# Second attention: score matmuls of 64 rows in two row groups, exponentials of two heads in one instruction, one ring of three banks for everything else

## The chip, the cores and the metric

The kernel runs on one core of a Trainium2 chip. The metric is the device time of one execution, in microseconds (us). A measurement of this kernel can tell a difference of some 0.3% from none.

## The reference

Input x has 4 batches of 1024 tokens with 128 features, all in float32. Four blocks follow one another, each added to x after a layer norm of x: a first attention with relative positions (8 heads), a feed-forward with a choice of two of eight experts, the second attention, and the same feed-forward again. The change is in the second attention. It has 16 query heads of 8 features and one key and one value head that all of them share:

```python
q = x @ Wq + bq
k = x @ Wk + bk
v = x @ Wv + bv
q = q.reshape(b, t, NUM_HEADS, HEAD_DIM)
scores = jnp.einsum('bthd,bsd->bhts', q, k) / jnp.sqrt(jnp.float32(HEAD_DIM))
mask = jnp.tril(jnp.ones((t, t), dtype=scores.dtype))
scores = scores * mask - 10000000000.0 * (1.0 - mask)
probs = jax.nn.softmax(scores, axis=-1)
out = jnp.einsum('bhts,bsd->bthd', probs, v)
out = out.reshape(b, t, NUM_HEADS * HEAD_DIM)
return out @ Wo + bo
```

## The kernel before, in words

**Layout.** The kernel is one program with five engine streams: SyncE (`sync`, line 343), GpSimd called POOL (445), TensorE (491), ScalarE (794) and VectorE (968). Each stream walks through the same lists of work units, `plan_a` for the first attention, `plan_f(0)`, `plan_b` for the second attention, `plan_f(1)`. A unit is a tuple such as `("b_s", b, g, ch, J, q)`. Engines meet through semaphores that count up. PSUM, TensorE's output memory, has eight banks of 512 float32 columns; `bank_free` holds for each bank the semaphore value that says that its reader is done.

**How a head fits the array.** Each number of queries and keys is split into a high part in float32r and a low rest, so that products of float32r matmuls come out in float32 accuracy. A head takes 32 of 128 partitions: 8 rows each for the products high times high, low times high and high times low, and two rows for the row maximum that is taken off. A group g has four heads q = 0 to 3 on partitions 32q to 32q+31. There are 4 batches b with 4 groups g, 16 head groups in all. The query tile `Q` holds all four heads of a group. The key tile `K` has four copies for each batch, one for each q, in which only the 32 partitions of q are filled and all others are zero (line 462 zeroes the tile once, lines 932 to 942 fill the blocks on ScalarE). So a matmul over all 128 rows gives the scores of head q alone.

**The units of a head group.** `b_in` (692) projects 512 tokens by three matmuls into bank 7, for g = 0 to 3 the queries, for g = 4 the keys. ScalarE takes the bank out twice, as `y` with bias and scale and as `yh` in float32r (lines 927 and 931); VectorE makes the mix of high and low parts in `b_in2` (1303 to 1317). `b_keys` copies the key blocks. `b_vals` (704) makes the values. `b_max` (712) makes scores for 128 queries of head q against up to 512 keys, into one of banks 0, 1, 2 in turn; VectorE reduces each to a row maximum (1328 to 1343), with a custom instruction that adds the causal mask where the tile has the diagonal, with a plain reduction elsewhere. There are 48 a group. `b_shift` and `b_shift2` (1344 to 1364) put the negated maxima into the spare rows of `Q` through PE transposes in bank 7. `b_s` (735) makes the scores the other way round, 128 keys (J) against up to 512 queries (half ch), into one of banks 3, 4, 5 in turn; ScalarE takes the exponential into `P`, a ring of `NP` = 7 tiles (943 to 952); POOL zeroes the upper triangle of the 128 diagonal columns where J is in the half (479 to 487). There are 48 of these a group too, four for each of twelve (ch, J), and eight of the twelve have a diagonal. `b_pv` (747) multiplies the four heads' `P` with the values in four matmuls of 128 rows and 32 columns, which write the four partition quadrants of bank 6. Columns of ones beside the eight of the values give the sum of the exponentials in the same matmul. `b_norm` copies the sums out on ScalarE, `b_norm2` (764, 1365) transposes them in bank 7 and VectorE divides. After the fourth group `b_out` and `b_out2` apply the output projection, also in bank 7. Layer norm pieces (`ln_turn`) and gate logits (`gt_logits`) of the next feed-forward run inside the stage, in bank 7.

**The order.** `plan_b` (165 to 234) writes the order by hand. `finish(n)` is the main list of head group n: three scores, then the value product of the key tile before, then the fourth score. `prepare(n+1)` is the side list: projections and maxima of the next group. The first `AHEAD` = 15 maxima of the group after that are kept to cover `b_shift` and `b_shift2` in `chain`. A loop (226 to 232) puts side units between main units so that both lists end together, by prices that stand in `cost` and `price`, one side unit at a time:

```python
            while i >= 4 and side and spent * total < goal * done:
                h = side.pop(0)
                out.append(h)
                spent += cost(h)
```

`first(b)` is the projection of the keys and of group 0 of batch b, spread into the side list of the last group of the batch before. For b = 0 it runs alone at the start of the stage, and then all maxima of group 0.

## Time and profile before

| what | value |
|---|---|
| median of 3 runs | 2920.83 us (2916.55 to 2924.42) |
| profiled execution, its own time | 2921.59 us |
| its span, first to last instruction | 2919.9 us |
| granted TensorE clock, mean | 0.952 of full speed |
| busy TensorE / VectorE / ScalarE / POOL | 2631.4 / 2041.6 / 1656.7 / 355.0 us |
| exponentials of the second attention (L952) | 768, 327.7 us |
| maximum matmuls (L721), score matmuls (L741) | 768 and 768 |

How to read it. Busy time of an engine is the union of its instructions' records. TensorE's matmuls overlap in the records, so that a busy TensorE is not an array at its peak: how far apart two matmuls start says what one costs. Times on the timeline count from the first instruction of the span. PE is TensorE's matmul, PEld its weight load, DVE is VectorE, ACT is ScalarE. L741 is line 741 of the kernel. A tile `ps` is PSUM, `r_K`, `r_Q`, `r_P`, `r_mx` are the tiles of the text above.

### The profile page before, as it was taken

How to read it: one execution, taken by the hardware profiler on the slowest of the kernel's cores; microseconds unless marked ns; L12 is line 12 of the kernel's file. 1: busy time of each engine (PE TensorE's matmuls, PEld its weight loads, DVE VectorE, ACT ScalarE, POOL GpSimd, SP SyncE). 2: the span in 40 equal slices, each digit the busy share in tenths (PEclk: the TensorE clock that was granted, in tenths of full speed). 3: DMA queues.
4: the chain of work that ended last, by engine and by line, in shares of the span. 5: the costliest groups of instructions: out<-in, count | busy, mean ns of one | idle time of the engine just before them, and what ended most of it. 6: DMA issues, size and time to landing. Idle time of an engine off the chain costs nothing.

```text
span 2919.9 us, 45160 instructions
## 1 busy us (share of the span) xinstructions
PE 2631.4 (90%) x14496; PEld 2047.8 (70%) x14496; DVE 2041.6 (70%) x5231; ACT 1656.7 (57%) x3430; POOL 355.0 (12%) x782
## 2 busy tenths in 40 slices
PE   2899999999999999999997079988998989998998
PEld 1688788888888888888886067765555555554777
DVE  3576776767767677677664078869777776773887
ACT  2566666666666666666664044544666656565454
POOL 0000000000000000000000123321221221222344
PEclk9999999999999999999999589978999999999999
DMA  2655556566655566556663100000000000000000
GB/s 84 206 203 205 183 200 209 200 214 207 211 205 201 205 214 214 205 195 205 214 208 110 51 6 1 1 1 1 1 1 1 1 1 1 1 1 1 9 8 15
DMA packets 98467, 321.63 MB, mean 110 GB/s; under 512 B 11556, under 2 KB 25508, under 8 KB 98020
## 3 DMA queue, kind: packets, MB, share of 16 engines
q1 hardware_dynamic: 98234, 318.74, 31.9%
q8 instruction: 119, 1.95, 0.3%
q14 instruction: 114, 0.93, 0.1%
HBM read 158.53 MB, written 157.29 MB: 108 GB/s over the span
## 4 chain that ended last, share of the span: by engine, by line
PE 77%; DVE 11%; ACT 5%; SPq 3%; issue 3%; DMA 1%; POOL 0%; DVEq 0%; ACTq 0%; POOLq 0%
PE ps L238 7%; PE ps L240 7%; PE ps L239 7%; PE ps L608 7%; PE ps L583 5%; PE ps L582 5%; PE ps L721 4%; PE ps L759 4%; PE ps L621 4%; PE ps L623 4%; PE ps L622 4%; PE ps L653 4%; PE ps L741 4%; PE ps L654 4%; PE ps L655 4%
## 5 line engine op out<-in xcount | busy, mean ns | idle before, releaser
L874 ACT ACTIVATE a_Ph<-ps 128x512 fp32r<-128x512 f32 x512 | 305.9, 597 | 474.5 <-PE ps L608 474.4
L1177 DVE CUSTOM_DVE_ANT_0 a_sp<-ps,a_sp 128x1024 f32<-128x1024 f32 x256 | 313.3, 1224 | 184.8 <-PE ps L240 178.9
L952 ACT ACTIVATE r_P<-ps 128x512 f32<-128x512 f32 (+3 forms) x768 | 327.7, 491 | 187.5 <-PE ps L741 183.2
L1183 DVE TENSOR_TENSOR a_Pl<-ps,a_Ph 128x512 fp32r<-128x512 f32 x512 | 349.3, 682 | 10.1 <-ACT a_Ph L874 9.8
L582 PE MATMUL ps<-a_fa,a_ua 128*128 128x384 f32 (+2 forms) x960 | 327.2, 353 | 5.0 <-DMA a_ub<-a_ua 2.6
L903 ACT ACTIVATE r_y<-ps 128x256 f32<-128x256 f32 x512 | 194.4, 385 | 220.9 <-PE ps L655 215.0
L867 ACT ACTIVATE a_sp<-a_sp,a_nm 128x1024 f32<-128x1024 f32 x256 | 295.0, 1152 | 29.4 <-DVE a_nm L1177 29.3
L608 PE MATMUL ps<-ident,a_sp 128*128 128x128 f32 x2048 | 309.0, 273 | 0.0
L653 PE MATMUL ps<-r_Wh,p_xh 128*128 128x512 f32 x512 | 223.0, 436 | 92.1 <-DVE r_Wl L1212 44.6
L721 PE MATMUL ps<-r_K,r_Q 128*128 128x512 f32 (+3 forms) x768 | 281.9, 402 | 18.0 <-DVE r_mx L1339 12.6
L608 PEld LDWEIGHTS ps<-ident,a_sp 128*128 128x128 f32 x2048 | 250.7, 141 | 61.6 <-issue 0.4
L583 PE MATMUL ps<-a_fb,a_ub 86*128 86x384 f32 (+2 forms) x960 | 290.9, 318 | 0.0
L1339 DVE CUSTOM_DVE_ANT_0 ps<-ps,maskq 128x256 f32<-128x256 f32 (+3 forms) x512 | 244.8, 506 | 54.2 <-PE ps L721 53.3
L741 PE MATMUL ps<-r_Q,r_K 128*128 128x512 f32 (+3 forms) x768 | 253.0, 374 | 30.2 <-ACT r_P L952 28.4
L859 ACT ACTIVATE a_rt<-ps 128x384 f32<-128x384 f32 x512 | 251.2, 491 | 10.5 <-PE ps L583 9.6
L721 PEld LDWEIGHTS ps<-r_K,r_Q 128*128 128x128 f32 x768 | 144.8, 198 | 157.9 <-DVE r_mx L1339 80.9
L473 POOL TENSOR_TENSOR r_acc<-r_acc,r_yk 128x256 f32<-128x256 f32 x256 | 189.4, 740 | 333.7 <-DVE r_yk L1244 322.8
L621 PE MATMUL ps<-a_Ph,a_nath 128*128 128x512 f32 x512 | 214.0, 418 | 15.9 <-DVE a_Pl L1183 15.9
L485 POOL TENSOR_SCALAR_AFFINE_SELECT r_P<-r_P 128x128 f32<-128x128 f32 x512 | 152.2, 307 | 556.3 <-ACT r_P L952 547.7
L1343 DVE TENSOR_REDUCE r_mx<-ps 128x1 f32<-128x512 f32 x256 | 176.2, 688 | 50.6 <-PE ps L721 49.3
L654 PE MATMUL ps<-r_Wl,p_xh 128*128 128x512 f32 x512 | 209.9, 410 | 0.0
L655 PE MATMUL ps<-r_Wh,p_xl 128*128 128x512 f32 x512 | 209.5, 409 | 0.0
(203 smaller groups left out, 5631.0 us busy)
## 6 DMA issues: line engine op xcount, KB each, us to landing
scr<-a_rt SPq DMA_DIRECT2D x256, 576.0 KB, 3.1
a_sp<-scr SPq DMA_DIRECT2D x256, 512.0 KB, 4.4
a_wc<-wsp SPq DMA_DIRECT2D x24, 512.0 KB, 5.5
wsp<-a_wc SPq DMA_DIRECT2D x8, 512.0 KB, 4.6
a_ub<-a_ua SPq DMA_DIRECT2D x64, 44.0 KB
x<-in_q SPq DMA_DIRECT2D x4, 512.0 KB, 15.9
wst<-in_w1t SPq DMA_DIRECT2D x8, 256.0 KB
out<-x SPq DMA_DIRECT2D x4, 512.0 KB, 3.2
```

The costliest lines, as they stand in the source:

```text
L582: e.matmul(out, self.ua[:, s, side, qs], self.fa[:, base + a:base + z], start=True, stop=False)
L583: i = e.matmul(out, self.ub[:, s, side, qs], self.fb[:, base + a:base + z], start=False, stop=True)
L608: i = e.transpose(ps[:, 4 + j % 2, 128 * k:128 * k + 128], self.sp[:, (4 * qd + k) % NSP, 128 * j:128 * j + 128], ident[:, :])
L621: e.matmul(OB, self.nath[:, s, j, :], self.Ph[:, slot, :], start=j == 0, stop=False)
L653: e.matmul(hb, self.xh[:, cs], self.Wh[:, k, :], start=True, stop=False)
L654: e.matmul(hb, self.xh[:, cs], self.Wl[:, k, :], start=False, stop=False)
L655: e.matmul(hb, self.xl[:, cs], self.Wh[:, k, :], start=False, stop=True).then_inc(S["f_mm"], 1)
L721: e.matmul(ps[:, bank, 0:w], self.Q[:, b % 2, g, 128 * I:128 * I + 128], self.K[:, b % 2, q, 512 * part:512 * part + w], start=True, stop= ...
L741: e.matmul(ps[:, bank, off:512], self.K[:, b % 2, q, 128 * J:128 * J + 128], self.Q[:, b % 2, g, 512 * ch + off:512 * ch + 512], start=Tru ...
L952: e.activation(self.P[:, pt, off:512], ps[:, bank, off:512], ACT.Exp).then_inc(S["b_exp"], 1)
L1177: e.tensor_tensor_reduce(out=w, in0=ps[:, 2:4, :].rearrange("p a n -> p (a n)"), in1=w, scale=-1.0, scalar=3e38, op0=ALU.add, op1=ALU.min, ...
L1183: e.tensor_tensor(self.Pl[:, n % 3, :], ps[:, 4 + n % 2, :], self.Ph[:, n % 3, :].bitcast(F32), ALU.subtract).then_inc(S["p_lo"], 1)
```

## The change

The kernel after differs in the second attention and in what prepares it:

1. **Keys.** `K` has `KV` = 2 copies for each batch instead of 4. Copy v holds the keys in the 32-partition blocks q with q % 2 = v, and zeros in the others. VectorE writes the mixed keys into a new tile `Kf`, and POOL makes both copies by a multiplication with a mask column (`lowmask`), two instructions of 512 columns for each half of a batch. The zeroing of `K` and ScalarE's `b_keys` go.
2. **Matmuls.** A maximum or score matmul of head q contracts 64 rows: partitions 0 to 63 for q = 0, 1, and 64 to 127 for q = 2, 3. The maxima go in the order q = 0, 2, 1, 3, so that neighbours are in different row groups. The width and the number of matmuls stay.
3. **Scores in pairs.** A unit `b_s` has two heads, pr and pr + 2, in banks 2 and 3 (pr = 0) or 4 and 5 (pr = 1). One ACTIVATE takes the exponential of both banks, `P` has 4 slots of two tiles, and POOL masks both tiles in one instruction. The order in `finish` is pair, pair, value product of the key tile before.
4. **Ring.** `b_max`, `b_in`, `b_vals`, `b_shift2`, `b_norm2`, `b_out` and `b_out2` take banks 0, 1, 7 in turn, in the order of the plan. `ln_turn` and `gt_logits` stay in bank 7. A `b_in2` is put off until its bank or its result is wanted. The side list gives two maxima at a time.
5. **Projection.** ScalarE reads the bank once, and multiplies by a mask column with a bias that has been multiplied beforehand, so that `yh` has the high part only in the rows that need it. VectorE takes it from the bank itself. The scale 1/sqrt(8) is applied to the weights once, in `b_prepare`.

```diff
-NP = 7
+NP = 4
+KV = 2
...
-        m = [("b_max", b, g, I, q, part) for I in range(7, -1, -1) for q in range(4) for part in range(1 + I // 4)]
-        q = [(u, b, g + 1, half) for u in ("b_in", "b_in2") for half in range(2)] if g < 3 else first(b + 1) if b + 1 < B else []
+        m = [("b_max", b, g, I, q, part) for I in range(7, -1, -1) for part in range(1 + I // 4) for q in (0, 2, 1, 3)]
+        q = [("b_in", b, g + 1, half) for half in range(2)] if g < 3 else first(b + 1) if b + 1 < B else []
...
-                r += [("b_s", b, g, ch, J, q) for q in range(3)] + prev + [("b_s", b, g, ch, J, 3)]
+                r += [("b_s", b, g, ch, J, 0), ("b_s", b, g, ch, J, 1)] + prev
...
-            while i >= 4 and side and spent * total < goal * done:
-                h = side.pop(0)
-                out.append(h)
-                spent += cost(h)
+            while i >= 2 and side and spent * total < goal * done:
+                for h in side[:2] if [v[0] for v in side[:2]] == ["b_max"] * 2 else side[:1]:
+                    out.append(side.pop(0))
+                    spent += cost(h)
...
+    ring, at, held, done = (0, 1, 7), 0, {}, []
+    for u in out:
+        shares = u[0] in ("b_in", "b_vals", "b_max", "b_shift2", "b_norm2", "b_out", "b_out2")
+        bank = ring[at % 3] if shares else 7 if u[0] in ("ln_turn", "gt_logits") else None
+        while bank in held or held and u[0] == "b_max" and [v for v in held.values() if v[2] in (u[2], 4)]:
+            done.append(held.pop(next(iter(held))))
+        done.append(u + (bank,) if shares else u)
+        at += shares
+        if u[0] == "b_in":
+            held[bank] = ("b_in2",) + u[1:] + (bank,)
...
+                        for v in range(KV):
+                            e.tensor_scalar(self.K[:, b % 2, v, os], self.Kf[:, half, :].bitcast(F32),
+                                            self.lowmask[:, 2 + v:3 + v], None, ALU.mult).then_inc(S["b_keys"], 1)
...
-                        e.affine_select(out=self.P[:, pt, off:off + 128], in_=self.P[:, pt, off:off + 128],
-                                        compare_op=ALU.is_ge, fill=0.0, pattern=[[1, 128]], channel_multiplier=-1,
+                        e.affine_select(out=self.P[:, slot, :, off:off + 128], in_=self.P[:, slot, :, off:off + 128],
+                                        compare_op=ALU.is_ge, fill=0.0, pattern=[[0, 2], [1, 128]], channel_multiplier=-1,
...
-                e.matmul(ps[:, bank, 0:w], self.Q[:, b % 2, g, 128 * I:128 * I + 128],
-                         self.K[:, b % 2, q, 512 * part:512 * part + w], start=True, stop=True).then_inc(S["b_mmm"], 1)
+                rows = slice(32 * (q - q % KV), 32 * (q - q % KV + KV))
+                e.matmul(ps[:, bank, 0:w], self.Q[rows, b % 2, g, 128 * I:128 * I + 128],
+                         self.K[rows, b % 2, q % KV, 512 * part:512 * part + w], start=True, stop=True).then_inc(S["b_mmm"], 1)
...
+                for k in range(2):
+                    bank, q = 2 + 2 * pr + k, pr + 2 * k
+                    rows = slice(32 * (q - q % KV), 32 * (q - q % KV + KV))
+                    e.wait_ge(*free[bank])
+                    i = e.matmul(ps[:, bank, off:512], self.K[rows, b % 2, q % KV, 128 * J:128 * J + 128],
+                                 self.Q[rows, b % 2, g, 512 * ch + off:512 * ch + 512], start=True, stop=True)
+                    free[bank] = S["b_exp"], nst
+                i.then_inc(S["b_smm"], 1)
...
-                e.activation(self.P[:, pt, off:512], ps[:, bank, off:512], ACT.Exp).then_inc(S["b_exp"], 1)
+                e.activation(self.P[:, slot, :, off:512], ps[:, bank:bank + 2, off:512], ACT.Exp).then_inc(S["b_exp"], 1)
...
-                e.activation(self.y[:, k, :], ps[:, 7, :], ACT.Identity, bias=self.bq[:, g:g + 1],
-                             scale=DB ** -0.5 if g < 4 else 1.0).then_inc(S["b_y"], 1)
...
-                e.activation(self.yh[:, k, :], self.y[:, k, :], ACT.Copy).then_inc(S["b_yh"], 1)
+                e.activation(self.yh[:, k, :], ps[:, bank, :], ACT.Identity, bias=self.bl[:, g:g + 1],
+                             scale=self.lowmask[:, m:m + 1]).then_inc(S["b_yh"], 1)
...
-                e.scalar_tensor_tensor(dst, self.yh[:, k, :].bitcast(F32), self.lowmask[:, m:m + 1], self.y[:, k, :],
-                                       ALU.mult, ALU.add).then_inc(S["b_y2"], 1)
+                e.scalar_tensor_tensor(dst, ps[:, bank, :], self.bq[:, g:g + 1], self.yh[:, k, :].bitcast(F32),
+                                       ALU.add, ALU.subtract).then_inc(S["b_y2"], 1)
```

## Rows read from the trace of the kernel before

**Rows 1.** Timeline of the head: start us, length us, engine, line, tiles

```profile
1949.90 0.73 PE L238 MATMUL ps<-p_xh,r_wh 128*128 128x512 f32 x1
...
1966.17 4.29 PE L721 MATMUL ps<-r_K,r_Q 128*128 128x512 f32 x7
```

**Rows 2.** Windows view: engines' busy us (instructions), clock, DMA share, GB/s, by stretch

```profile
core 0: us, PE busy (x) PEld busy (x) DVE busy (x) ACT busy (x) POOL busy (x), PEclk, DMA share, GB/s
1949.00:1966.00 17.00, 12.38 (x42) 9.14 (x41) 3.30 (x5) 10.06 (x16) 0.00 (x0) 0.50 0.00 0
1970.00:2006.00 36.00, 33.18 (x97) 19.32 (x96) 34.22 (x108) 7.61 (x14) 1.31 (x5) 0.71 0.00 1
2006.00:2636.00 630.00, 575.06 (x3445) 336.02 (x3443) 476.56 (x1617) 394.88 (x865) 141.76 (x475) 0.97 0.00 1
2636.00:2670.00 34.00, 27.07 (x166) 11.35 (x166) 2.26 (x8) 22.62 (x53) 9.09 (x32) 1.00 0.00 1
```

**Rows 3.** Timeline of the tail, one key tile of full width

```profile
2657.62 1.06 PE L759 MATMUL ps<-r_P,r_V 128*32 128x512 f32 x8
...
2658.62 0.97 PE L741 MATMUL ps<-r_Q,r_K 128*128 128x512 f32 x3
2659.16 2.07 ACT L952 ACTIVATE r_P<-ps 128x512 f32<-128x512 f32 x4 [0.55 <-PE ps L741]
...
2659.81 0.50 PE L741 MATMUL ps<-r_Q,r_K 128*128 128x512 f32 x1 [0.22 <-ACT r_P L952]
...
2660.24 1.06 PE L759 MATMUL ps<-r_P,r_V 128*32 128x512 f32 x8
```

**Rows 4.** Waits view, 2006 to 2636 us: total us, times, longest us

```profile
ACT r_P L952 <- PE ps L741: 175.8, 154, 4.2
...
DVE ps L1339 <- PE ps L721: 53.3, 70, 3.2
...
DVE r_mx L1343 <- PE ps L721: 47.6, 53, 3.2
```

**Rows 5.** Timeline around a value product with maxima beside it

```profile
2627.19 0.28 PE L721 MATMUL ps<-r_K,r_Q 128*128 128x256 f32 x1
...
2627.40 1.06 PE L759 MATMUL ps<-r_P,r_V 128*32 128x512 f32 x8
2627.51 0.43 DVE L1339 CUSTOM_DVE_ANT_0 ps<-ps,maskq 128x256 f32<-128x256 f32 x1
...
2628.40 0.50 PE L721 MATMUL ps<-r_K,r_Q 128*128 128x256 f32 x2
...
2628.82 0.43 DVE L1339 CUSTOM_DVE_ANT_0 ps<-ps,maskq 128x256 f32<-128x256 f32 x1 [0.82 <-PE ps L721]
```

**Rows 6.** TensorE groups by form, 2006 to 2670: busy us, mean ns, idle before

```profile
L759 PE MATMUL ps<-r_P,r_V 128*32 128x512 f32 x768 | 104.0, 613 | 2.0 <-ACT r_P L952 0.7
```

**Rows 7.** Groups of ScalarE by form, 2006 to 2670 us

```profile
L952 ACT ACTIVATE r_P<-ps 128x512 f32<-128x512 f32 x384 | 206.3, 599 | 129.2 <-PE ps L741 128.5
...
L952 ACT ACTIVATE r_P<-ps 128x128 f32<-128x128 f32 x124 | 30.6, 276 | 7.0 <-PE ps L741 4.9
...
L931 ACT ACTIVATE r_yh<-r_y 128x512 fp32r<-128x512 f32 x33 | 20.8, 631 | 1.1
...
L941 ACT ACTIVATE r_K<-r_yk 32x512 fp32r<-32x512 f32 x24 | 15.0, 624 | 0.4
```

**Rows 8.** Costliest groups of the page: an exponential of 1024 columns

```profile
L867 ACT ACTIVATE a_sp<-a_sp,a_nm 128x1024 f32<-128x1024 f32 x256 | 295.0, 1152 | 29.4 <-DVE a_nm L1177 29.3
```

**Rows 9.** Groups of VectorE, 2006 to 2636 us

```profile
L1339 DVE CUSTOM_DVE_ANT_0 ps<-ps,maskq 128x256 f32<-128x256 f32 (+1 forms) x472 | 224.6, 504 | 54.2 <-PE ps L721 53.3
L1343 DVE TENSOR_REDUCE r_mx<-ps 128x1 f32<-128x512 f32 x231 | 159.0, 688 | 48.8 <-PE ps L721 47.6
```

**Rows 10.** Groups of POOL, 1949 to 2670 us

```profile
L485 POOL TENSOR_SCALAR_AFFINE_SELECT r_P<-r_P 128x128 f32<-128x128 f32 x512 | 152.2, 307 | 556.3 <-ACT r_P L952 547.7
```

**Rows 11.** Timeline of POOL before the first feed-forward

```profile
1607.04 1.26 POOL L461 TENSOR_TENSOR wst<-wst,wr 128x512 f32<-128x512 f32 x1 [1604.70 <-DMA wr<-in_w1r]
```

224 lines of the change are left out of this document (109 added, 115 removed).

## The prediction, as it was made before the kernel ran

> **What bounds the kernel now.** I read the page first, for where the second attention lies, then the windows view of its stretches, the waits in the long one, the groups of VectorE, and the timeline of two spots. The stage runs from the first query and key projection at 1949.9 us [rows 1] to about 2670 us, 720 of 2919.9 us; nothing else of the program is changed by more than a microsecond or two. It has four stretches [rows 2]. A head of projections (1949 to 1966). A filling phase (1970 to 2006), in which TensorE has only row-maximum matmuls to do and VectorE reduces them: it is busy 34.22 of 36 us. The long stretch, 630 us, in which 15 of the 16 head groups get scores, exponentials and value products while the next group's maxima are made. And a tail of 34 us with the last group's scores and hardly any VectorE work.
>
> In the long stretch VectorE is busy 476.56 us, ScalarE 394.88, and TensorE 575.06; but TensorE's records overlap, so its 91% is not array time. The array's demand comes from start to start: a group of three score matmuls of 512 columns takes 0.97 us where one takes 0.50, so (0.97 - 0.50)/2 = 0.235 us each [rows 3]. One value product (four heads, eight records) keeps the array 1.0 us, from 2657.62 to 2658.62. Per head group the maxima and the scores each have 36 full widths of 512 columns (4608 columns for each of four heads), so 72 x 0.235 = 16.9 us; value products have 9 full widths, 9.0 us; the projections (7.5 matmuls, 1.8 us), four sets of four transposes (each at most as long as a value product, so up to 4) and small ones give some 6. That is 32 us of 630/15 = 42.0. VectorE's demand is 476.6/15 = 31.8 us. Neither engine is full: both lose about 10 us a group to each other. The waits view says how: VectorE stood 53.3 + 47.6 us for maximum matmuls, ScalarE 175.8 us for score matmuls [rows 4]. The timeline shows the usual case [rows 5]: a value product starts at 2627.40 and holds TensorE until 2628.40, VectorE finishes the maxima that were ready, and gets the next at 2628.82, after 0.82 us idle. VectorE's whole idle time is 630 - 476.6 = 153.4 us, 10.2 a group, 0.85 for each of its 12 value products. So the stage is bound by an in-order TensorE that alternates between banks freed by two other engines, with TensorE and VectorE nearly level in demand.
>
> **The change, part by part.**
>
> **Matmuls of 64 rows.** The 1536 maximum and score matmuls stay as many and as wide, but neighbours use rows 0-63 and 64-127 and different banks. If such a pair runs at once, the 16.9 us fall to 8.5 at best. No row of this trace has two row groups. The nearest is the value product, whose four heads use four column groups: 613 ns a record and eight records in 1.06 us [rows 3, 6], so they do run at once. Bounds: 8.5 us off a group, or nothing, or less than nothing by switches; I take 8.5 for the scores' half and for the maxima count it as hidden, since a pair there starts together only where both banks are free. The Trainium skill, page TensorE: Matmul & The Clock Gate, section on packing small matmuls, has row groups start about 4 ns apart; by it the full 8.5 us would go, which is the same sum, and no row here shows it.
>
> **Mode switches.** In the rows a value product's 1.0 us is all that can hold a switch in and out, and there are still 12 a group. New are switches between 64-row matmuls and full ones: about 8 other units a group. I price two switches at 0.1 us each, 1.6 us a group, from a full-width score before a value product (2659.81 to 2660.24, 0.43 us) [rows 3]: over its 0.235 that is 0.2, part of it a wait; zero is the other end. It lies on TensorE, which then has 32 - 8.5 + 1.6 = 25 us of demand and room for it. The Trainium skill, page TensorEngine Tiling (Array Packing), section Key Properties, says that changing the tiling mode drains the engine. By it with TensorE still the bound, 15 x 1.6 = 24 us would be given back.
>
> **Exponentials in pairs.** 768 become 384. By length, 599 ns for 512 columns and 276 for 128 [rows 7] give 0.84 ns a column and 0.168 us fixed, so 1.03 us for 1024. Four in a row took 2.07 us, spaced (2.07 - 0.60)/3 = 0.49 [rows 3], so a lower bound is 0.92; the upper is 1.15, the 1024-wide exponential of the first attention [rows 8]. I take 1.03. Also off ScalarE go the second copy of each projection (631 ns x 40) and the 32 copies of keys (624 ns) [rows 7], 45 us in the stage. ScalarE is at 63% in the long stretch, so none of this is on the path by itself.
>
> **Four banks for scores, three for all else.** Scores wait for the exponential of the same pair one key tile earlier. Maxima keep three banks but share them with projections, transposes and outputs (some 10 turns a group), and are issued two at a time. What a projection holds: its bank until ScalarE's pass and VectorE's subtraction; VectorE waits for ScalarE, which may have one 1.03 us exponential ahead of it. Before it was covered by two units between them; now by two bank turns, two maxima of about 0.55 us (224.6 + 159.0 over 703) [rows 9]. I count 0.5 us x 2.5 a group.
>
> **Masks and keys on POOL.** The 512 masks of 307 ns [rows 10] become 256 of twice the elements: between 0.31 and 0.61, I take 0.45. It stands in the way of the eight diagonal value products of a group by 0.15 us at most, beside maxima that TensorE still has. The key copies, 16 on 512 columns, at most the 1.26 us of the two-input subtraction [rows 11]: POOL is 77% idle [rows 2], but masks queue behind them, and a value product behind those: 6 halves x 2.5 = 15 us as the outer bound in the long stretch, 0 the other; I take 3, since the wait of POOL comes with maxima still to do. The memset of the key tile at the first feed-forward's start goes; POOL waits there anyway, so nothing; neither does the scaling of the weights, one VectorE instruction and one ScalarE wait in the first feed-forward, once.
>
> **The steady sum.** What VectorE does per group is unchanged (the projection's subtraction reads a bank in place of a tile). The question is its idle time. From the last pair of maxima before a value product to the next that VectorE gets: 0.235 for a pair of scores, 1.0 for the product, 0.42 from issue to VectorE's start (2628.40 to 2628.82) [rows 5], 1.66 us. The stock at that point is up to three maxima, 3 x 0.55 = 1.6, where now two or fewer were left. So 0.1 to 0.4 idle a product; I take 0.22, 2.6 us a group, and 2.4 for projections, keys and the group's end, where the shift is made of the last maxima. That is 5.0 in place of 10.2: 15 x 5.2 = 78 us less. ScalarE's demand becomes some 22 us a group (12 pairs of full width at 1.03, four each of 384, 256 and 128 columns at 0.81, 0.60 and 0.38, and 3 for projections and sums), TensorE's 25: both stay below the 36.8 that VectorE then needs.
>
> **Tail.** There a key tile of full width takes 2.62 us (2657.62 to 2660.24), of which ScalarE idles 0.55 [rows 3]: a third bank is not enough over a value product. With two pairs the exponentials can follow each other, 2 x 1.03 = 2.06. Six full tiles x 0.56 = 3.4; I take 3.
>
> **Head.** From 1949.90 to the first maximum at 1966.17 [rows 1] are 16.3 us, one projection after the other through one bank. With three banks, four projections of three matmuls and the values can run on, about 12 us: 4 less, from 0 to 6.
>
> Sum: 78 + 3 + 4 = 85 us off the profiled execution's 2921.6; it is 0.8 above the median of 2920.83. Forecast 2836.
>
> **Bounds of the sum.** Best: VectorE idles only as in the filling phase, 1.78 us on 34.22 [rows 2], 25 us in the long stretch, 128 saved there, 10 at the ends: 2783. Worst of this case: it is 80% busy, 596 us, 34 saved and 3 at the ends: 2884.
>
> **Rivals.**
> **VectorE saturated.** The stock of three covers the product nearly always: 2783 to 2800. For it: the filling phase. Against: the products are 1.0 us and the widths of 128 reduce in a third of the time of a full one.
> **Row groups one after the other, or switches that eat the gain.** TensorE keeps 32 us plus up to 1.6 of demand, level with VectorE. Only the paired exponentials and fuller stock help; idle falls to 7.5 us a group, 15 x 2.7 = 40 saved, 5 at the ends: 2876. For it: no row shows row groups together. Against: column groups do.
> **Nothing moves.** The shared ring's waits (0.5 us and more at 10 turns) give back what the pairs bring: 2915 to 2925.
> **Slower: TensorE's clock.** A less busy array might be granted 1.2 GHz for long. It was granted 0.97 in the long stretch, 0.71 in the filling phase [rows 2]. At half clock 25 us of demand become about 49, over the 42.0 of now. With a share f of half clock a group takes 36.8 + 12.2 f: it decides from f = 0.43; at 0.6 it is 44.1, 32 us worse in all, less 7 at the ends: 2946. Against: the tail, with scores and products only and gaps between them, ran at 1.00.
>
> **How the numbers follow.** The forecast 0.60, VectorE saturated 0.12, row groups in series 0.16, nothing moves 0.04, clock 0.08. The first three are faster, 0.88. The range goes from the best bound to a little over the third case, 2782 to 2888, and leaves out the clock and the no-change case. 0.3% (9 us) is about what a measurement of this kernel can tell from no change.
>
> **What would show it.** Right: pairs of score matmuls that start within tens of ns; VectorE at 83 to 90% of the long stretch, which is about 550 us; 384 exponentials, about 1.03 us at full width; full tiles of the tail at about 2.1 us; a granted clock as before. Wrong: a pair spaced 0.235 us, VectorE's waits for maximum matmuls above 80 us still, long waits of VectorE for the projection's ScalarE pass, or a clock under 0.8.

## The result, and the profile after

The change makes the kernel **slower**: 3016.49 us (median of 4 runs, 3014.02 to 3023.82) against 2918.69 for the kernel before beside it, ratio 1.034 with an interval of 1.031 to 1.036. Forecast was 2836 us, faster by 2.9%. The profiled execution took 3014.02 us, its span is 3011.6 us, and the mean granted TensorE clock fell from 0.952 to 0.897. The clock has two levels here, 1.2 and 2.4 GHz, so that a mean of 0.75 is half of the time at the lower one; that share is called the half-clock share below.

The clock by slices of the page, kernel after. The second attention lies in the 26th to the 37th of the 40 slices:

```profile
PEclk9999999999999999999995799956976778768999
```

The windows view of the kernel after answers to [rows 2]: filling phase, long stretch, tail, then one head group, and the same units of the next batch:

```profile
core 0: us, PE busy (x) PEld busy (x) DVE busy (x) ACT busy (x) POOL busy (x), PEclk, DMA share, GB/s
1970.00:2006.00 36.00, 29.66 (x67) 15.93 (x68) 29.70 (x95) 2.84 (x3) 0.00 (x0) 0.50 0.00 0
2006.00:2730.00 724.00, 636.31 (x3447) 311.74 (x3447) 483.37 (x1617) 336.13 (x453) 114.62 (x252) 0.75 0.00 1
2730.00:2756.00 26.00, 23.36 (x170) 8.88 (x172) 3.03 (x8) 20.03 (x27) 6.41 (x16) 0.93 0.00 1
2151.60:2188.40 36.80, 31.54 (x216) 14.83 (x214) 29.09 (x92) 20.62 (x28) 6.40 (x16) 1.00 0.00 1
...
2352.40:2398.40 46.00, 42.35 (x215) 19.59 (x214) 29.52 (x92) 20.82 (x28) 6.45 (x16) 0.67 0.00 1
```

And the windows view of the kernel before, of the group with the same units as the last two:

```profile
2128.90:2166.30 37.40, 35.14 (x218) 20.31 (x216) 29.23 (x92) 23.52 (x53) 9.64 (x32) 1.00 0.00 1
```

Three things are in these lines. The long stretch is 724 us where 630 were before and 550 forecast, at a clock of 0.75 where it was 0.97: half of it at 1.2 GHz. The same head group takes 36.80 us at full clock and 46.00 us at 0.67, while what VectorE, ScalarE and POOL have to do in it is the same (29.09 and 29.52 us, 20.62 and 20.82, 6.40 and 6.45); only TensorE's records grow. And at full clock this group takes 36.80 us against 37.40 before: the change gains 0.6 us there, not 5.2.

One group doesn't stand for all. Timed in both traces from the first exponential of a group to the first of the next, with the half-clock share in brackets:

| head groups, in order | before, us | after, us |
|---|---|---|
| 3 and 11 | 46.4 (0.15), 47.0 (0.15) | 42.8 (0.16), 44.2 (0.15) |
| 4, 8 and 12 | 37.7, 37.8, 37.7 (0 each) | 36.8 (0), 46.0 (0.67), 37.6 (0.09) |
| 6, 10 and 14 | 46.4, 45.9, 48.0 (0.07, 0.07, 0.14) | 63.2, 63.6, 63.7 (0.76, 0.70, 0.86) |
| 15 | 31.3 (0) | 26.3 (0) |

Where the clock is the same, the change gains between 0.9 and 5.0 us a group. Groups 6, 10 and 14 lose 16 to 18 us each, with the highest half-clock shares. In the order of the plan they are the groups among whose units stand the layer norm pieces and gate logits of the next feed-forward, which keep to bank 7, now one of the ring's three. With 128-row matmuls and nearly the full clock (the first experiment below) they still take 53.5, 56.3 and 51.5 us, so a part of their loss is not the clock.

The groups by form, kernel after, from 1950 to 2760, answer to [rows 6, 7, 9, 10, 11]:

```profile
L964 ACT ACTIVATE r_P<-ps 128x1024 f32<-128x1024 f32 x192 | 191.4, 1023 | 186.5 <-PE ps L767 185.3
L744 PE MATMUL ps<-r_K,r_Q 64*128 64x512 f32 x384 | 161.3, 592 | 52.9 <-DVE r_Q L1329 34.9 <-DVE r_mx L1352 5.7 <-DVE p_xl L1039 3.2
L786 PE MATMUL ps<-r_P,r_V 128*32 128x512 f32 x768 | 121.3, 709 | 0.7 <-ACT r_P L964 0.6
L509 POOL TENSOR_SCALAR_AFFINE_SELECT r_P<-r_P 128x256 f32<-128x256 f32 x256 | 102.6, 407 | 611.2 <-ACT r_P L964 609.1
L501 POOL TENSOR_SCALAR r_K<-r_Kf,lowmask 128x512 fp32r<-128x512 f32 x16 | 24.8, 1564 | 62.1 <-DVE r_Kf L1329 62.1
```

The single prices were right where a row had been near: 1023 ns for two heads' exponentials (1.03 taken), 407 ns for a double mask (0.45 taken). A value product's record grew from 613 [rows 6] to 709 ns; in the two like groups above it is 605 ns at full clock and 757 at 0.67, so that goes with the clock. The key copies are dearer than their upper bound, 1.56 us for at most 1.26.

The waits from 2006 to 2730, kernel after, answer to [rows 4]:

```profile
ACT r_P L964 <- PE ps L767: 322.6, 197, 19.3
DVE ps L1352 <- PE ps L744: 112.5, 92, 4.4
...
PEld ps L744 <- DVE r_Q L1329: 46.0, 24, 3.3
...
DVE r_mx L1356 <- PE ps L744: 43.3, 57, 1.9
```

VectorE stands 156 us for maximum matmuls where it stood 101, and ScalarE 323 where it stood 176. A new wait is TensorE's for L1329, the projection's step on VectorE, in whose bank the next maximum has to go. The timeline shows it once, at full clock:

```profile
2153.77 0.39 PE L249 MATMUL ps<-p_xl,r_wh 128*128 128x512 f32 x1
2154.33 0.50 PE L744 MATMUL ps<-r_K,r_Q 64*128 64x512 f32 x2
2154.44 0.78 ACT L953 ACTIVATE r_yh<-ps,r_bl,lowmask 128x512 fp32r<-128x512 f32 x1 [1.72 <-PE ps L250]
2156.07 0.74 DVE L1329 SCALAR_TENSOR_TENSOR r_Q<-ps,r_bq,r_yh 128x512 fp32r<-128x512 f32 x1
2156.86 0.51 PE L744 MATMUL ps<-r_K,r_Q 64*128 64x512 f32 x2 [0.59 <-DVE r_Q L1329]
2157.39 1.29 DVE L1356 TENSOR_REDUCE r_mx<-ps 128x1 f32<-128x512 f32 x2 [0.59 <-PE ps L744]
```

TensorE gives two maxima at 2154.33 and the next two only at 2156.86, right after L1329 ends; VectorE then waits 0.59 us for them. The two matmuls of a line start together (x2 in 0.50 us, as long as one), so the row groups do run at once.

The tail came out as predicted, or better. The timeline between two full-width value products in it:

```profile
2748.10 2.98 ACT L964 ACTIVATE r_P<-ps 128x1024 f32<-128x1024 f32 x3
2749.74 1.06 PE L786 MATMUL ps<-r_P,r_V 128*32 128x512 f32 x8
2751.27 2.95 ACT L964 ACTIVATE r_P<-ps 128x1024 f32<-128x1024 f32 x3 [0.19 <-PE ps L767]
2751.66 1.06 PE L786 MATMUL ps<-r_P,r_V 128*32 128x512 f32 x8
```

From one product to the next it is 1.92 us, against 2.62 before [rows 3] and 2.06 forecast.

### The profile page after: what moved, and what is told of

Its sections match the earlier page's. It is cut to its first block, busy times and chain, and to the rows that moved or that the text cites. A ratio compares the mean times of both kernels' runs of the same rounds, so it can differ in the third digit from the quotient of the medians.

```text
span 3011.6 us, 43744 instructions
## 1 busy us (share of the span) xinstructions
PE 2684.2 (89%) x14496; PEld 2015.9 (67%) x14496; DVE 2049.5 (68%) x5234; ACT 1584.7 (53%) x2974; POOL 322.6 (11%) x541
## 3 DMA queue, kind: packets, MB, share of 16 engines
q8 instruction: 117, 1.92, 0.3%
## 4 chain that ended last, share of the span: by engine, by line
PE 77%; DVE 11%; ACT 4%; SPq 3%; issue 3%; DMA 1%; POOL 0%; DVEq 0%; POOLq 0%; ACTq 0%
PE ps L248 7%; PE ps L250 7%; PE ps L249 7%; PE ps L632 7%; PE ps L744 6%; PE ps L786 5%; PE ps L607 4%; PE ps L606 4%; PE ps L645 4%; PE ps L647 4%; PE ps L646 4%; PE ps L677 3%; PE ps L678 3%; PE ps L679 3%; PE ps L767 3%
## 5 line engine op out<-in xcount | busy, mean ns | idle before, releaser
L964 ACT ACTIVATE r_P<-ps 128x1024 f32<-128x1024 f32 (+3 forms) x384 | 298.3, 809 | 329.6 <-PE ps L767 328.0
L744 PE MATMUL ps<-r_K,r_Q 64*128 64x512 f32 (+3 forms) x768 | 287.7, 518 | 79.9 <-DVE r_Q L1329 40.0
L744 PEld LDWEIGHTS ps<-r_K,r_Q 64*128 64x128 f32 x768 | 146.8, 242 | 264.8 <-DVE r_mx L1352 79.8
L786 PE MATMUL ps<-r_P,r_V 128*32 128x512 f32 (+3 forms) x1536 | 208.4, 623 | 5.5 <-ACT r_os L970 4.6
L248 PE MATMUL ps<-p_xh,a_gah 128*128 128x512 f32 x512 | 206.2, 403 | 2.0 <-DVE a_nm L1191 2.0
L1256 DVE SCALAR_TENSOR_TENSOR r_yk<-ps,p_comb,r_y 128x256 f32<-128x256 f32 x384 | 182.9, 480 | 34.0 <-ACT r_y L929 19.7
```

The lines of the kernel that those rows point to most:

```text
L248: e.matmul(out, lh, rh, start=True, stop=False)
L744: e.matmul(ps[:, bank, 0:w], self.Q[rows, b % 2, g, 128 * I:128 * I + 128], self.K[rows, b % 2, q % KV, 512 * part:512 * part + w], start= ...
L786: i = e.matmul(ps[32 * q:32 * q + 32, 6, off:512], self.V[:, b % 2, J, :], self.P[:, (got - 2 + q % 2) % NP, q // 2, off:512], start=J == ...
```

## The experiments: which part costs

Eighteen kernels ran. Ratios are to the kernel before on the same chip, with 95% intervals; the clock is the mean of the one profiled execution, whose time can lie at the edge of the others (for 128 rows it was the fastest of four, 2944.6 us).

| kernel | rows | us | ratio (interval) | clock |
|---|---|---|---|---|
| after | 64 | 3016.5 | 1.034 (1.031 to 1.036) | 0.897 |
| after with 128-row matmuls | 128 | 2952.4 | 1.011 (1.009 to 1.013) | 0.952 |
| after, neighbours in one row group | 64 | 3072.9 | 1.052 (1.050 to 1.055) | 0.883 |
| before with 64-row matmuls alone | 64 | 3022.0 | 1.034 (1.032 to 1.036) | 0.896 |

**128 rows, all else of the change kept.** The key tile has four copies again. For room, `yh` and `Kf` lie over tiles of the feed-forward, with the waits that this needs. POOL makes twice as many key copies, and neighbouring matmuls can't run at once any more.

```diff
-KV = 2
+KV = 4
...
-        self.yh = sb("yh", [128, 2, 512], F32R)
+        self.yh = self.y[:, :, :].bitcast(F32R)
...
-        self.Kf = sb("Kf", [128, 2, 512], F32R)
+        self.Kf = self.yk[:, :, :].bitcast(F32R)
```

> The changed kernel with the score and maximum matmuls back at 128 rows (four zero-padded key copies), everything else of the change kept: pairs of heads per exponential, two maxima at a time, the ring of banks 0, 1, 7. Theory A (score pairs that run at once leave the array idle, and the clock is granted at 1.2 GHz for that): the granted clock of the stage goes back to 0.93 or more, and the time to 2830 to 2900, since a fit of the 15 head groups of the changed kernel against their share of half clock gave 34.8 us at full clock against 39.8 before. Theory C (the shared ring's waits make the loss and the gaps): the clock stays under 0.85 and the time at 2990 to 3050.

Measured: 2952.38 us, 1.0109 (1.0088 to 1.0131). The windows view of its long stretch:

```profile
2008.00:2664.00 656.00, 581.76 (x3474) 347.61 (x3472) 483.88 (x1623) 337.83 (x456) 133.30 (x264) 0.96 0.00 1
```

With 128 rows the clock is back at 0.96, and two thirds of the loss are gone. But 1.1% stays, so the rest of the change costs something as well, and the 2830 to 2900 us that theory A expected did not come. Its ground was a line fitted through the 15 groups, 34.8 us at full clock against 39.8. Such a line mixes groups of different work: it prices the half clock at some 32 us a group, where like groups give 13.9 (worked out below).

**The 64-row matmuls with neighbours in the same row group.** Heads in the order 0, 1, 2, 3, so that neighbours cannot run at once.

```diff
-        m = [("b_max", b, g, I, q, part) for I in range(7, -1, -1) for part in range(1 + I // 4) for q in (0, 2, 1, 3)]
+        m = [("b_max", b, g, I, q, part) for I in range(7, -1, -1) for part in range(1 + I // 4) for q in range(4)]
...
-                    bank, q = 2 + 2 * pr + k, pr + 2 * k
+                    bank, q = 2 + 2 * pr + k, 2 * pr + k
```

> The changed kernel, with the heads ordered 0, 1, 2, 3, so that neighbouring matmuls of 64 rows share a row group and can't run at once. Theory A (idle time of the array): the clock comes back to 0.93 or more and the time is as that of the kernel with 128 rows, within 1%. Theory B (a matmul of 64 rows counts for less, whether or not it overlaps): the clock stays at 0.7 to 0.8 and the time is above the changed kernel's 3016, at 3030 to 3100, since the matmuls now take their full time at the low clock. Theory C: little moves, 3016 to 3050.

Measured: 3072.87 us, 1.0525 (1.0501 to 1.0549), clock 0.883. This is theory B's range. Running two at once is worth 56 us here, a part of which may be the somewhat lower clock. It is not the overlap that lowers the clock: without it, it is lower still.

**The row change alone, on the kernel before.** The lines shown are those of the maxima; the score matmuls are changed in the same way, and the heads go in the order 0, 2, 1, 3.

```diff
-        self.K, self.V = sb("K", [128, 2, 4, L], F32R), sb("V", [128, 2, 8, 32])
+        self.K, self.V = sb("K", [128, 2, 2, L], F32R), sb("V", [128, 2, 8, 32])
...
-                e.matmul(ps[:, bank, 0:w], self.Q[:, b % 2, g, 128 * I:128 * I + 128],
-                         self.K[:, b % 2, q, 512 * part:512 * part + w], start=True, stop=True).then_inc(S["b_mmm"], 1)
+                rows = slice(64 * (q // 2), 64 * (q // 2) + 64)
+                e.matmul(ps[:, bank, 0:w], self.Q[rows, b % 2, g, 128 * I:128 * I + 128],
+                         self.K[rows, b % 2, q % 2, 512 * part:512 * part + w], start=True, stop=True).then_inc(S["b_mmm"], 1)
```

> The kernel before, with the matmuls of 64 rows in two row groups alone (head order 0, 2, 1, 3, two key copies), one exponential a head, the old rings of three banks. Theories A and B: the clock of the stage falls below 0.88 and the time is above before, 2940 to 3020. Theory C (the ring): no ring here, so the time is at or below before's 2919, down to 2870, with the clock above 0.93.

Measured: 3022.01 us, 1.0339 (1.0315 to 1.0363), clock 0.896. The row change alone gives the whole loss; the clock of its long stretch is 0.76. The parts don't add: rows alone 3.4%, the rest alone 1.1%, both together 3.4%. Under the 64-row clock the rest costs nothing more.

## The experiments: the clock

**A filler of 128 rows.** One more matmul of 128 rows and the same width ahead of each maximum matmul, its product overwritten.

```diff
+                e.matmul(ps[:, bank, 0:w], self.Q[:, b % 2, g, 128 * I:128 * I + 128], self.K[:, b % 2, q % KV, 512 * part:512 * part + w],
+                         start=True, stop=True)
                 e.matmul(ps[:, bank, 0:w], self.Q[rows, b % 2, g, 128 * I:128 * I + 128],
```

> The changed kernel with one more matmul of 128 rows and the same width in front of each maximum matmul, into the same bank, overwritten by it: 768 more matmuls, work that nobody needs. It adds 36 x 0.235 = 8.5 us of array time a head group at full clock. Theory A and B: the clock of the stage rises to 0.9 or more and the kernel gets faster than 3016 in spite of more work, 2880 to 2960. Theory C: the clock is not what costs, and the time goes up to 3030 to 3120.

Measured: 3612.46 us, 1.237 (1.234 to 1.239), clock 0.816. Both theories failed. The timeline of TensorE shows what was overlooked, at half clock and at full clock:

```profile
2199.58 0.80 PE L744 MATMUL ps<-r_K,r_Q 128*128 128x512 f32 x1
2200.31 0.79 PE L746 MATMUL ps<-r_K,r_Q 64*128 64x512 f32 x1
2201.03 0.79 PE L744 MATMUL ps<-r_K,r_Q 128*128 128x512 f32 x1
...
2206.97 0.50 PE L746 MATMUL ps<-r_K,r_Q 64*128 64x512 f32 x1
2207.39 0.50 PE L744 MATMUL ps<-r_K,r_Q 128*128 128x512 f32 x1
2207.83 0.50 PE L746 MATMUL ps<-r_K,r_Q 64*128 64x512 f32 x1
```

Neighbours of different tile shape start 0.72 us apart at half clock and 0.43 at full clock, for 512 columns that take 0.235 between equals. The filler had brought far more changes of shape: counted in the traces over the stage, some 1850 against 510 in the kernel after. So it says nothing of the clock by itself. Why its clock was low as well (0.60 from 2052 to 3349) was not found.

**A filler that changes no shape**, and its control on the kernel before: each maximum matmul issued twice, with the same rows and to the same bank.

```diff
+                e.matmul(ps[:, bank, 0:w], self.Q[rows, b % 2, g, 128 * I:128 * I + 128],
+                         self.K[rows, b % 2, q % KV, 512 * part:512 * part + w], start=True, stop=True)
                 e.matmul(ps[:, bank, 0:w], self.Q[rows, b % 2, g, 128 * I:128 * I + 128],
```

> The kernel after the change, with each of the 768 maximum matmuls of 64 rows issued twice in the same row group and to the same bank: twice the array work of the maxima, and no new change of tile shape between neighbours (the filler before it doubled those changes, and cannot speak for the clock alone). If the granted clock follows how much of the time the array works, whatever the rows, it rises above the 0.897 of after, and the time stays at 3016 or falls, as low as 2960. If work in 64 rows is what the clock does not count as full work, the clock stays at 0.88 to 0.90 and the time only gains the added columns, 768 x 0.23 to 0.46 us = 177 to 353 us of array work of which a third to a half shows: 3070 to 3190 us.

> The kernel before, with each maximum matmul of 128 rows issued twice: the control of the 64-row run with doubled maxima, which cost 0.6% over after and brought its clock from 0.897 to 0.915. If there the array's added work was paid for by clock that came back, the same doubling here, where the clock is 0.95 already, has little to win back and costs more: 3 to 6%, 3010 to 3090 us, clock 0.95 or above. If the array's time is simply not what bounds either kernel, it costs about the same 0.6% here: 2930 to 2945.

Measured: on after 3034.05 us, 1.0381 (1.0359 to 1.0403), clock 0.915; on before 2992.02 us, 1.0243 (1.0228 to 1.0258), clock 0.962. The long stretches, in the windows view of the one and of the other kernel:

```profile
2014.00:2765.00 751.00, 674.57 (x4175) 382.41 (x4173) 489.15 (x1622) 340.02 (x455) 115.02 (x252) 0.83 0.00 1
```

```profile
2000.00:2700.00 700.00, 667.71 (x4158) 445.42 (x4155) 495.14 (x1622) 407.17 (x867) 143.44 (x480) 0.99 0.00 1
```

The same number of matmuls more, 768, cost the kernel before 72 us and the kernel after 18 us (in the profiled executions the long stretch grows by 70 and by 27 us). In the second the clock of the stretch rises from 0.75 to 0.83, in the first there was little to win, from 0.97 to 0.99. This is a strong sign that the clock costs the time and doesn't merely go with it. It is not a proof: TensorE of the kernel after also waits more, and may hide more of the added work. The first run fell between its two ranges, the control cost less than the 3 to 6% expected.

**Streams without pauses.** Five streams of 512 columns on TensorE alone, put after the second attention of the kernel before.

```diff
+        for kind, count in ((0, 800), (1, 800), (2, 1600), (0, 400), (3, 600)):
+            for k in range(count):
+                half = 0 if kind == 1 else k % 2
+                rows = slice(0, 128) if kind == 0 or kind == 3 and k % 2 else slice(64 * half, 64 * half + 64)
+                e.matmul(ps[:, 0 if kind == 1 else k % 2, :], self.K[rows, 1, 0, 0:128],
+                         self.Q[rows, 1, 3, 0:512], start=True, stop=True)
```

> The kernel before, with five streams of matmuls of 512 columns put on TensorE alone after the second attention, while the other engines wait: 800 of 128 rows, 800 of 64 rows in one row group, 1600 of 64 rows in alternating row groups, 400 of 128 rows, 600 alternating between 128 and 64 rows. If the clock falls for work in 64 rows as such: 1.00 in the first and fourth stream, 0.5 in the second, and between in the third, where two run at once. If it falls for pauses of the array: 1.00 in the first four and below 1 in the fifth, where each change of shape leaves a gap. A change of shape costs 0.2 us by the filler run: the fifth takes 600 x 0.43 = 258 us at full clock, against 600 x 0.22 = 132 us without it.

Windows view, one line in the middle of each stream: 128 rows; 64 rows in one row group; 64 rows in two; 128 rows; 128 and 64 in turn:

```profile
2700.00:2870.00 170.00, 170.00 (x734) 137.82 (x733) 0.00 (x0) 0.00 (x0) 0.00 (x0) 1.00 0.00 1
2880.00:3055.00 175.00, 175.00 (x755) 139.22 (x754) 0.00 (x0) 0.00 (x0) 0.00 (x0) 1.00 0.00 1
3065.00:3240.00 175.00, 175.00 (x1509) 140.12 (x1508) 0.00 (x0) 0.00 (x0) 0.00 (x0) 1.00 0.00 1
3250.00:3335.00 85.00, 85.00 (x367) 68.91 (x366) 0.00 (x0) 0.00 (x0) 0.00 (x0) 1.00 0.00 1
3345.00:3590.00 245.00, 245.00 (x579) 106.94 (x579) 0.00 (x0) 0.00 (x0) 0.00 (x0) 1.00 0.00 0
```

Both theories failed: the clock was full in all five (one execution). Neither 64 rows as such nor changes of shape as such lower it. The prices are clean here: 170/734 = 0.232 us for a 128-row matmul, 175/755 = 0.232 for a 64-row one in one row group, 175/1509 = 0.116 in two, and 245/579 = 0.423 where the shape changes each time, so 0.19 us for one change in such a stream. It can be less in the kernel: in the trace of after, at full clock, a 64-row matmul that follows one of 128 rows and 512 columns starts 0.32 us after it (middle value of 16), 0.09 over the 0.23.

**The same with pauses.** TensorE fills one bank while VectorE reduces the other, as the maxima do, 250 times for each of six kinds.

```diff
+PACED = ((None, 2), (1, 2), (2, 2), (None, 1), (1, 1), (2, 4))
...
+                if p >= 2:
+                    e.wait_ge(S["z_dve"], p - 1)
+                for k in range(each):
+                    half = 0 if halves is None else k % halves
+                    rows = slice(0, 128) if halves is None else slice(64 * half, 64 * half + 64)
+                    i = e.matmul(ps[:, 2 * half + p % 2, :], self.K[rows, 1, 0, 0:128],
+                                 self.Q[rows, 1, 3, 0:512], start=True, stop=True)
```

> The kernel before, with TensorE and VectorE alone after the second attention, in step as in the maxima: VectorE takes the maximum of a bank of 512 columns (0.69 us) while TensorE fills the other one, 250 times each of six kinds: two matmuls of 128 rows a bank; two of 64 rows in one row group; two of 64 rows in two row groups; one of 128 rows; one of 64 rows; four of 64 rows in two row groups. The streams without pauses kept the full clock whatever their rows. If, with pauses, rows count: the second kind falls to half clock where the first, with the same 0.46 us of matmuls a period, keeps more. If only the time counts in which the array has a matmul: the second is like the first, the third (0.23 us a period) like the fourth, the sixth like the first.

Windows view, one line a kind, in that order: two of 128 rows for a reduction; two of 64 in one row group; two of 64 in two; one of 128; one of 64; four of 64 in two:

```profile
2700.00:2870.00 170.00, 152.46 (x449) 66.67 (x448) 147.85 (x226) 0.00 (x0) 0.00 (x0) 1.00 0.00 0
2890.00:3120.00 230.00, 230.00 (x462) 114.19 (x461) 159.05 (x230) 0.00 (x0) 0.00 (x0) 0.50 0.00 0
3130.00:3325.00 195.00, 164.69 (x476) 67.79 (x474) 152.42 (x236) 0.00 (x0) 0.00 (x0) 0.50 0.00 0
3335.00:3520.00 185.00, 170.11 (x236) 67.68 (x235) 157.87 (x235) 0.00 (x0) 0.00 (x0) 0.50 0.00 0
3535.00:3720.00 185.00, 177.40 (x236) 66.86 (x235) 162.54 (x236) 0.00 (x0) 0.00 (x0) 0.50 0.00 0
3740.00:3920.00 180.00, 152.24 (x908) 67.33 (x904) 147.73 (x227) 0.00 (x0) 0.00 (x0) 1.00 0.00 1
```

Two matmuls of 128 rows for each reduction ran at 2.4 GHz. Two of 64 rows in one row group, which began at 2.4 GHz right after them, fell to 1.2 GHz and stayed there. What differs between the first kind and the second is the rows alone. The sixth kind, four of 64 rows, began at 1.2 GHz and came back to 2.4. With pauses between, two matmuls of 64 rows do not keep the clock as two of 128 rows do; without pauses (the streams before) they do. And a fall costs pace: in the second kind a reduction came every 1.00 us, in the first every 0.75, for at half clock the two matmuls have become the bound. The third to fifth kind came after a stretch at half clock and stayed at it, the single matmul of 128 rows too; whether they would have held the full one from a start at it was not tried. All this is one execution, with the kinds in one order.

## The experiments: the 1.1% that is not the clock

| kernel (128 rows unless said) | us | ratio (interval) | clock |
|---|---|---|---|
| 128-row form, maxima in banks 0 and 1, rest in bank 7 | 3040.8 | 1.042 (1.040 to 1.043) | 0.943 |
| 128-row form, key copies on ScalarE | 2948.2 | 1.009 (1.007 to 1.011) | 0.946 |
| 64 rows, maxima four at a time | 3120.2 | 1.069 (1.067 to 1.071) | 0.871 |
| 128-row form, maxima one at a time | 2951.5 | 1.011 (1.009 to 1.012) | 0.951 |
| 64 rows, maxima one at a time | 3022.3 | 1.034 (1.033 to 1.036) | 0.893 |
| before, exponentials in pairs in the last group | 2921.7 | 1.000 (0.999 to 1.001) | 0.951 |
| 128-row form, bank by last use | 3027.3 | 1.037 (1.035 to 1.040) | 0.943 |
| 64 rows, bank by last use | 3135.7 | 1.076 (1.072 to 1.079) | 0.872 |
| before, shared ring alone | 2923.7 | 1.001 (1.000 to 1.002) | 0.951 |
| 128-row form, projection's step one unit earlier | 2931.4 | 1.004 (1.003 to 1.005) | 0.951 |

**Maxima in a ring of two.**

```diff
-        bank = ring[at % 3] if shares else 7 if u[0] in ("ln_turn", "gt_logits") else None
+        bank = (0, 1)[at % 2] if u[0] == "b_max" else 7 if shares or u[0] in ("ln_turn", "gt_logits") else None
```

> The 128-row form of the change (first experiment, 2952 us, 1.011 of before) with only the maxima in a ring of banks 0 and 1, and bank 7 for the projections, the transposes and the output products, as a bank of their own. If the shared ring of three is what costs the 1.1% that is left (maximum matmuls wait 34 + 22 us for a bank that a projection holds until VectorE has read it twice), the time falls to 2900 to 2930. If the third bank for the maxima matters more, VectorE waits for maximum matmuls more than the 78 + 27 us of the first experiment, and the time is 2960 to 3020.

3040.76 us: the third bank is worth 3% to the maxima. With one bank fewer, sharing is the better choice.

**Key copies on ScalarE**, out of POOL's queue with the masks.

```diff
-                            e.tensor_scalar(self.K[:, b % 2, v, os], self.Kf[:, half, :].bitcast(F32),
-                                            self.lowmask[:, 2 + v:3 + v], None, ALU.mult).then_inc(S["b_keys"], 1)
...
+                    e.activation(self.K[:, b % 2, v, os], self.Kf[:, half, :].bitcast(F32), ACT.Copy,
+                                 scale=self.lowmask[:, 2 + v:3 + v]).then_inc(S["b_keys"], 1)
```

> The 128-row form of the change with the masked copies of the keys made by ScalarE (Copy with a per-row factor) and not by GpSimd, where 32 copies of 1.56 us stand in one queue with the causal masks that the value products wait for. If this queue is what costs the 1.1%: the three long head groups at the start of a batch (53.5, 56.3 and 51.5 us against 46.4, 45.9 and 48.0 before) come down by 4 to 7 us each, and the time to 2930 to 2940. If not, ScalarE gets 32 x 0.6 = 19 us more work, which it has room for (it waits 283 us for score matmuls): 2945 to 2965.

2948.20 us, the intervals of the two overlap: the queue of POOL does not cost the 1.1%.

**Maxima four at a time, 64 rows** (`side[:4]` in place of `side[:2]` in the loop of `plan_b`).

> The kernel after the change with the maxima put between the score pairs and value products four at a time and not two at a time: nothing else is moved. That takes away up to 12 of some 24 pairs that stand alone in a head group, each with up to two changes between 64-row and 128-row tiles. If those changes (about 0.2 us each at full clock, 0.3 at half) are a large part of the loss, 12 x 2 x 0.2 us x 16 groups = 77 us of array time go and the time falls to 2940 to 2990. If the loss is the granted clock, it stays within 1% of 3016, the clock within 0.01 of 0.897, or is worse because four maxima meet a ring of three banks.

3120.17 us, the clock at 0.871. The run was meant to take changes of shape away, but did not: the score pairs between which the maxima stand have 64 rows as well, and the long stretch has 514 changes where the kernel after has 513. What it shows is the ring: four maxima meet three banks, VectorE stands 229 us for maximum matmuls where it stood 156, and the clock falls further. The order in twos is not the fault either:

**Maxima one at a time** (`side[:1]`), with 128 and with 64 rows.

> The 128-row form of the change (first experiment, 2952 us), with the maxima put into the order one at a time, as before the change, and not in twos. With four at a time the 64-row kernel lost 3.5% more, and with a ring of two banks the 128-row one lost 3%: theory: how the maxima meet their ring of banks (the third unit of a ring that projections and transposes share waits on VectorE) costs the 1.1% that is left. Then single maxima give 2915 to 2935. Rival: the order in twos costs nothing at a ring of three, and the loss is the projection's bank, held until VectorE has read it twice: 2945 to 2960.

> The kernel after the change, 64 rows, with the maxima one at a time and not in twos. If the 64-row loss is the clock, the time moves only as the 128-row kernel beside it does (some 20 to 30 us down): 2985 to 3015. If each unit that stands alone pays for changing the tile shape (0.2 us twice at full clock), up to 24 more changes of shape a head group come in: 3030 to 3100.

2951.52 and 3022.33 us: nothing with 128 rows, 0.2% slower at most with 64. Here too the changes of shape hardly grow, to 533. So neither run prices them; the count does. The kernel before has 356 in its long stretch, all between 128x128 and 128x32 tiles. The 157 that the kernel after has more, at 0.09 to 0.19 us, are 14 to 30 us of TensorE's time at full clock, an estimate, against 98 us lost: the smaller part.

**The bank by last use.**

```diff
-        bank = ring[at % 3] if shares else 7 if u[0] in ("ln_turn", "gt_logits") else None
+        bank = min(used, key=used.get) if shares else 7 if u[0] in ("ln_turn", "gt_logits") else None
...
+        if bank is not None:
+            used[bank] = at + (0 if u[0] == "b_max" else 4)
```

> The 128-row form with single maxima (2951.5 us, 1.0107 of before), with the bank of a unit chosen as the one whose last user is longest ago, where a projection, transposes or an output product count as four units later than a maximum: a maximum no longer meets in turn the bank that such a unit holds. If the shared ring in strict turn is what costs the 1.1% (the long groups at a batch's start wait for the bank of a projection and of the normalisation), the time falls to 2920 to 2935; the 6 us that the stage starts later (GpSimd's key copies) stay. If it stays at 2945 to 2955, the ring's turn is not it.

> The same choice of banks in the kernel after the change (64 rows, maxima in twos). If clock and ring are separate costs, it gains what the 128-row kernel gains, 15 to 30 us: 2985 to 3000, the clock within 0.01 of 0.897. If the array idles less and the clock comes back with it, more: 2950 to 2985 and a clock of 0.91 to 0.93.

Both expectations failed: 3027.28 and 3135.70 us. The maxima now avoid a bank that a projection or transposes had, but come back to the others too soon: counted in the order of the units, 48 of the 768 maxima get the bank of the unit right before them and 233 that of two units before, where the ring in turn always leaves two units between. By its time it is most of the ring of two again. The group of its maximum matmuls, with 128 rows, from 2000 to 2800 (what ended the idle time before them stands last):

```profile
L746 PE MATMUL ps<-r_K,r_Q 128*128 128x384 f32 (+1 forms) x731 | 278.4, 417 | 89.7 <-DVE r_mx L1362 36.1 <-DVE r_mx L1366 23.0 <-DVE r_Q L1339 19.1
```

**The shared ring alone, on the kernel before.** All units that the change puts into the ring take banks 0, 1, 7 in turn, bank 2 is unused, the rest is as before.

```diff
+    ring, at, done = (0, 1, 7), 0, []
+    for u in out:
+        shares = u[0] in ("b_in", "b_vals", "b_max", "b_shift2", "b_norm2", "b_out", "b_out2")
+        done.append(u + (ring[at % 3],) if shares else u)
+        at += shares
```

> The kernel before with one part of the change alone: maxima, projections, values, transposes and output products share a ring of the banks 0, 1 and 7 in strict turn (bank 2 is left unused), and everything else, 128 rows, single exponentials, single maxima, stays. If the ring is what costs the 1.1% of the 128-row form: 1.01 or more, 2950 to 2985 us, for here no paired exponentials give 5 us back at the end. If the ring is harmless: 2915 to 2925.

2923.71 us, 1.0007 (0.9997 to 1.0017): the ring alone is harmless. The bank that was taken from the maxima cost nothing as long as a projection let go of its bank after ScalarE's pass.

**The projection's step on VectorE one unit earlier**, on the 128-row form with single maxima.

```diff
         at += shares
+        if held and shares and u[0] != "b_in":
+            done.append(held.pop(next(iter(held))))
```

> The 128-row form with single maxima (2951.5 us, 1.0107 of before), with VectorE's step of a projection put one unit of the ring earlier: at present it stands right ahead of the unit that takes the projection's bank again, so that TensorE waits for it there and VectorE then for TensorE. The ring alone is harmless (1.0007). If the bank held by the projection is what costs the 1.1%: 2920 to 2935. If it stays at 2945 to 2955, the cost is in the score pairs and their four banks, or in the later start of the stage.

2931.36 us, 1.0041 (1.0029 to 1.0054), from 1.0107. The waits from 2006 to 2690, first without and then with the edit:

```profile
DVE ps L1360 <- PE ps L744: 74.7, 72, 3.5
...
PEld ps L744 <- DVE r_Q L1337: 37.6, 24, 2.6
...
DVE r_mx L1364 <- PE ps L744: 33.9, 70, 2.7
```

```profile
DVE ps L1362 <- PE ps L746: 71.0, 56, 5.1
PEld ps L746 <- DVE r_mx L1362: 55.9, 122, 1.8
```

TensorE's wait for the projection's step has gone from the list. Put off until its bank was wanted, the step stood right ahead of the maximum that had to wait for it. That was some 20 of the 31 us. The other 0.4% was not settled. The traces show where it lies: the first exponential comes at 2012.4 us against 2002.6 before, and groups 6, 10 and 14 take 50.3, 55.7 and 50.4 us against 46.4, 45.9 and 48.0, while most others are about as short as before or shorter. Whether it is the layer norm pieces and gate logits in the ring's bank 7 was not tried. POOL's key copies are a suspect for the start of the stage, but taking them off POOL gained nothing.

**Exponentials in pairs in the last head group alone**, on the kernel before: bank pairs (0,1), (2,3), (4,5), six slots.

```diff
+                    e.activation(self.P[:, pt - 1:pt + 1, off:512], ps[:, bank:bank + 2, off:512], ACT.Exp).then_inc(S["b_exp"], 2)
```

> The kernel before, 128 rows, with what gained in every form of the change and nothing else of it: exponentials of two heads in one instruction in the last head group alone, where the maxima are done and their three banks are free (three bank pairs, six slots for the exponentials). That group took 28.8 us before, 22.7 to 26.3 in the changed forms. Expected 4 to 6 us less, 2914 to 2917 us, ratio 0.998 with an interval that just about leaves 1 out; if the six slots hold ScalarE back (a second pair waits for the value product of the tile before), 0 to 3 us less.

2921.69 us, 1.0000 (0.9990 to 1.0009). The gain of the tail did not come over: the last group's exponentials took 30.0 us in the profiled execution, 28.7 before and 23.8 in the kernel after. There was no room for eight slots, and with six a pair waits for the value product of the tile before: ScalarE stood 7.7 us for value products. No version of these ran faster than the kernel before.

## Why the prediction was wrong

**The step that failed first is the weight of the clock.** The rival "Slower: TensorE's clock" named the mechanism, the place and nearly the price, and got 0.08. It put half clock at 12.2 us a head group; measured, the same units went from 36.80 to 46.00 us with the clock at 0.67, that is 66% of the time at half clock, so 9.2/0.66 = 13.9. It put the break-even at a share of 0.43 and the share measured was 0.5. So what failed is the chance given to it, and with it the line "a granted clock as before", more than its price. It was set aside with one sentence: "the tail, with scores and products only and gaps between them, ran at 1.00". But the tail of before had 128-row matmuls. The change takes half the rows out of every maximum and score matmul, and the paced run shows, in its first two kinds, that this alone can take the clock from 1.00 to 0.50. In [rows 2] the filling phase, where TensorE waits for VectorE, was already granted 0.71: it was the row to go by, for the change was to give TensorE more waiting of that kind. There the clock moved between both levels with 128-row maxima alone (1.00 from 1975 to 1980 us, 0.50 from 1985 to 1995). After, it is 0.50.

**The steady sum failed too, on its own.** The term is VectorE's idle time, 10.2 us a group, which was to fall to 5.0. In group 4, at full clock, it is 37.40 - 29.23 = 8.2 us before and 36.80 - 29.09 = 7.7 after. No group of the kernel after came down to 5.0; the lowest, group 15, has 6.5. And groups 6, 10 and 14 got longer at nearly the full clock too, as the 128-row form shows. Its long stretch is 656 us at 0.96, longer than the 630 before; it lacks the row groups, so it doesn't price the rest exactly. One part of the sum is found: "0.5 us x 2.5 a group", 1.25 us, for the projection's bank was too small. TensorE waited 46 us for it in the long stretch, 3.1 a group, and on the 128-row form an edit of a few lines that lets it go earlier brought 20 us.

**The two together.** Forecast for the long stretch was 550 us, it is 724, a miss of 174. The half-clock share is 0.50 where it was 0.06, so the clock takes 15 x 0.44 x 13.9 = 92 us. The other 82 are about the whole gain of 78 us that the steady sum promised: what some groups win at equal clock, groups 6, 10 and 14 seem to lose again. This is an estimate with the price of one kind of group, and the parts were not measured one by one.

**Mode switches.** The sum had two switches at 0.1 us for each of some eight units a group, 1.6 us. Measured is 0.19 us each in the stream (0.423 less 0.232) and 0.09 at the places of the kernel where one follows a 128-row matmul. The Trainium skill, page TensorEngine Tiling (Array Packing), section Key Properties, says that a change of tiling mode drains the engine; the traces agree in that a change takes time, and do not show by what. For the 157 changes more, 10.5 a group, that is 0.9 to 2.0 us: this term was about right.

**What was right.** Row groups run at once (0.116 us a matmul in the stream), and the kernel is 56 us faster for it than with neighbours in one row group. 1.03 us for a paired exponential was 1.023. The tail: 2.06 us a tile forecast, 1.92 measured. The head went the other way: 4 us less were forecast, and the first score came at 2005.7 us, 3.4 later than before (2002.3), with the filling phase at half clock. The marks set for "wrong" came true, VectorE's waits for maxima above 80 us and a clock under 0.8 in the stretch.
